# The first state of batches 1 to 7: its product with C moved from VectorE to ScalarE, behind the transposes, and the gate moved to step 1

## What is computed

```python
dA = jnp.exp(jnp.einsum('bti,is->btis', delta, A))
dBu = jnp.einsum('bti,bts->btis', delta * u, B_ssm)
def step(h, inp):
    dA_t, dBu_t, C_t = inp
    h = dA_t * h + dBu_t
    y_t = jnp.einsum('bis,bs->bi', h, C_t)
    return (h, y_t)
...
y = ys.transpose(1, 0, 2) + u * D_param
y = y * jax.nn.silu(z)
return y @ out_proj_w.T + residual
```

## Time and profile before

| what | us |
|---|---|
| median of 3 runs | 610.64 (609.68 to 610.68) |
| the profiled execution's own time | 611.13 |
| its span | 609.3 |
| DVE busy | 588.5 |
| PE busy | 542.0 |
| POOL busy | 494.1 |
| ACT busy | 455.0 |
| mean granted clock of PE | 0.969 of full speed |

### The profile page before, as it was taken

The page is one execution under the profiler, slowest core; times in us unless marked ns, Lnnn a source line. Parts: engine busy times, 40 slices in busy tenths (PEclk is TensorE's granted clock), DMA queues, the critical chain, the costliest instruction groups (busy, mean ns, idle before and its releaser), DMA issues.

```text
span 609.3 us, 11382 instructions
## 1 busy us (share of the span) xinstructions
PE 542.0 (89%) x3554; PEld 422.5 (69%) x3554; DVE 588.5 (97%) x852; ACT 455.0 (75%) x916; POOL 494.1 (81%) x389
## 2 busy tenths in 40 slices
PE   5999889898898998999989999899999797778887
PEld 2387766656787777877887777877777465657564
DVE  6999989999999999999999999999999998999997
ACT  1789697259857888579876698767985589969880
POOL 5693466569999799998999889998998967885784
PEclk9889798979999999999999999999999899988999
DMA  7430119725787887878868888688884455333364
GB/s 205 135 130 1 74 36 223 306 82 157 256 304 223 293 289 223 311 226 296 296 190 304 291 288 279 203 300 268 280 266 156 156 195 210 110 99 98 88 137 90
DMA packets 60893, 122.99 MB, mean 202 GB/s; under 512 B 8218, under 2 KB 41378, under 8 KB 53794
## 3 DMA queue, kind: packets, MB, share of 16 engines
q1 hardware_dynamic: 53826, 112.42, 54.7%
q0 software_dynamic: 6288, 9.52, 7.3%
q10 hardware_dynamic: 720, 0.33, 0.2%
HBM read 112.77 MB, written 9.47 MB: 201 GB/s over the span
## 4 chain that ended last, share of the span: by engine, by line
PE 50%; DVE 19%; ACT 16%; issue 13%; POOL 1%; DMA 1%; DVEq 0%; ACTq 0%; POOLq 0%
PE bank L1433 9%; PE bank L1584 8%; PE bank L1467 8%; DVE bank L1144 8%; PE bank L1598 6%; DVE h_sb L1161 6%; PE bank L1592 5%; ACT bank L515 3%; ACT dbu L531 3%; PE bank L1490 2%; ACT da L503 2%; PE bank L1482 2%; PE bank L1396 1%; PE bank L1565 1%; ACT L770 1%
## 5 line engine op out<-in xcount | busy, mean ns | idle before, releaser
L931 POOL TENSOR_TENSOR dbu<-du,xn_all 128x1024 f32<-128x1024 f32 x86 | 203.7, 2369 | 24.9 <-DVE bank L1144 21.5
L1144 DVE TENSOR_TENSOR_SCAN bank<-bank,dbu 128x512 f32<-128x512 f32 x170 | 207.4, 1222 | 0.8 <-ACT bank L515 0.2
L1161 DVE TENSOR_TENSOR h_sb<-bank,xh_all 128x512 f32<-128x512 f32 x240 | 159.6, 680 | 1.2
L515 ACT ACTIVATE bank<-delta,a_sb 128x512 f32<-128x512 f32 x170 | 116.7, 688 | 37.9 <-DVE h_sb L1161 37.2
L1433 PE MATMUL bank<-id_sb,h_sb 128*128 128x128 f32 x992 | 131.9, 277 | 10.9 <-DVE h_sb L1161 9.3
L1433 PEld LDWEIGHTS bank<-id_sb,h_sb 128*128 128x128 f32 x992 | 112.9, 143 | 21.6 <-DVE h_sb L1161 14.7
L1144 DVE TENSOR_TENSOR_SCAN bank<-da,bank 128x512 f32<-128x512 f32 x82 | 96.0, 1215 | 4.6 <-PE bank L1396 2.9
L1584 PEld LDWEIGHTS bank<-wd_sb,hid 117*128 117x128 f32 (+1 forms) x432 | 54.8, 191 | 49.2 <-DVE hid L1195 28.4
L1584 PE MATMUL bank<-wd_sb,hid 117*128 117x128 f32 (+1 forms) x432 | 64.1, 284 | 18.7 <-ACT xT L696 17.2
L915 POOL DMA_INDIRECT xs<-xn_rows,src x72 | 69.8, 970 | 12.5 <-issue 9.9
L531 ACT ACTIVATE dbu<-du_t,bc_sb 128x256 f32<-128x256 f32 x164 | 69.4, 496 | 6.3 <-PE bank L1396 3.4
(11 more groups left out here) (198 smaller groups left out, 893.8 us busy)
## 6 DMA issues: line engine op xcount, KB each, us to landing
xh_all<-b_rows SPq DMA_DIRECT2D x30, 1024.0 KB, 7.5
xn_all<-b_rows SPq DMA_DIRECT2D x25, 1024.0 KB
wgu_sb<-in_w_gu SPq DMA_DIRECT2D x72, 352.0 KB
wd_sb<-in_w_dn SPq DMA_DIRECT2D x72, 192.0 KB
y_slots<-ys SPq DMA_DIRECT2D x72, 64.0 KB
xn_rows<-xn_all SPq DMA_DIRECT2D x2, 1040.0 KB, 11.4
out<-x_sb SPq DMA_DIRECT2D x7, 256.0 KB, 7.0
x_sb<-in_x SPq DMA_DIRECT2D x2, 640.0 KB, 6.0
```

The costliest lines, as they stand in the source:

```text
L515: nc.scalar.activation(bank_of(b, m)[:, :], delta[b % 2][:, hf, :], ACT.Exp, scale=a_sb[:, hf, k:k + 1]).then_inc(s["da_rdy"], 1)
L931: nc.gpsimd.tensor_tensor(dbu[k % 2][:, :, :], du[b % 2][:, :, :], b_ring[c % 2][:, k % CH, :].unsqueeze(1).to_broadcast([P, NH, T]), ALU. ...
L1144: nc.vector.tensor_tensor_scan(at, da_of(n)[:, hf, :] if n in IN_SBUF else at, inp, 0.0, ALU.mult, ALU.add).then_inc(s["h_rdy"], 1)
L1161: nc.vector.tensor_tensor(h_sb[k % 2][:, hf, :], bank_of(b, 2 * k + hf)[:, :], row, ALU.mult).then_inc(s["p_rdy"], 1)
```

## The change

For step 0 of batches 1 to 7 (`BY_SCALAR`, n = 16b):

- The scan writes h_sb0 instead of its bank, and waits for that buffer at its start. The two products are not issued.
- PE turns the bare state into banks 2 and 3 with its first sums, and ACT multiplies the banks in place by C's column, four times 128x256 (`multiplied`), as the last work of its step 1. PE's sums of step 1 wait for that.
- The bank of such a step is free after its scan instead of after its product (`bank_read`).
- C's columns exist already for batches 6 and 7. For 1 to 5 PE turns them with four small transposes and ACT copies them (`own_columns`), in batch 0's step 7 and 8 for batch 1, and in front of one `slots_turn` of the batch before for the others.
- The gate stands in step 1, between its first scan with the expert product and its first product.
- On PE, the sums of steps 0 and 1 (issued in steps 1 and 2) stand behind gate and slots_turn in batches 1 to 5, and behind the next step's first dbu transposes in 6 and 7. In batch 6 the two halves of skip move from steps 1 and 2 to 2 and 3.

```diff
+        BY_SCALAR = [S * b for b in range(1, NB)]
+        def by_vector(m):
+            return m - sum(min(max(m - 2 * n, 0), 2) for n in BY_SCALAR)
+        def bank_read(eng, m):
+            if m > 0 and (m - 1) // 2 in BY_SCALAR:
+                wait(eng, "h_rdy", m)
+            else:
+                wait(eng, "p_rdy", by_vector(m))
...
-        SKIPPED = {6: (1, 2), 7: (2, 4)}
+        SKIPPED = {6: (2, 3), 7: (2, 4)}
+        COLUMN_TILE = {TILE[(b - 1) * S + (7 if b == 2 else 5)]: b for b in range(2, 6)}
...
-                wait(act, "p_rdy", freed(b, m))
+                bank_read(act, freed(b, m))
...
+                if g - 1 in BY_SCALAR:
+                    multiplied(g - 1)
...
+            def multiplied(n):
+                b, k = n // S, n % S
+                i0 = BY_SCALAR.index(n)
+                if 0 < b < 6:
+                    act.wait_ge(s["cc_rdy"], b)
+                for i in range(2):
+                    act.wait_ge(s["acc_mm"], 2 * n + i + 1)
+                    for t in (2 * i, 2 * i + 1):
+                        last = nc.scalar.activation(HT[i][:, t % 2, :], HT[i][:, t % 2, :], ACT.Copy,
+                                                    scale=bc_sb[b % 2][:, t, S + k:S + k + 1])
+                    last.then_inc(s["hc_rdy"], 1)
+            def own_columns(c):
+                act.wait_ge(s["cc_mm"], c)
+                at = XHB if c == 1 else XD
+                nc.scalar.activation(bc_sb[c % 2][:, :, S:S + 1], at[:, 2 * P:3 * P].rearrange("p (t c) -> p t c", t=TT)[:, :, S:S + 1],
+                                     ACT.Copy).then_inc(s["cc_rdy"], 1)
...
-                    wait(dve, "p_rdy", 2 * S * b + 1)
-                nc.vector.tensor_tensor_scan(at, da_of(n)[:, hf, :] if n in IN_SBUF else at, inp, 0.0,
+                    bank_read(dve, 2 * S * b + 1)
+                to = at
+                if n in BY_SCALAR:
+                    to = h_sb[k % 2][:, hf, :]
+                    wait(dve, "acc_mm", 2 * (n - 1))
+                nc.vector.tensor_tensor_scan(to, da_of(n)[:, hf, :] if n in IN_SBUF else at, inp, 0.0,
...
+                if b * S + k in BY_SCALAR:
+                    return
...
+                if k == 1:
+                    gate(b - 1)
                 product(b, k, 0)
...
-                if k == 0:
-                    gate(b - 1)
...
-                wait(pe, "p_rdy", 2 * (n + 1))
+                bank_read(pe, 2 * (n + 1))
...
+                    if n - 1 in BY_SCALAR:
+                        pe.wait_ge(s["hc_rdy"], 2 * BY_SCALAR.index(n - 1) + i + 1)
...
+                for t in range(TT):
+                    last = nc.tensor.transpose(at[:, 2 * P + t * 2 * S:2 * P + (t + 1) * 2 * S], bct_full[0:2 * S, t * P:(t + 1) * P],
+                                               id_sb[0:2 * S, 0:2 * S])
...
-                if k > 0:
+                if k > 2:
                     accumulate(g - 1)
                 if g + 1 in BY_PE:
                     dbu_turn(b, k + 1, (0,))
+                if k in (1, 2) and b > 5:
+                    accumulate(g - 1)
...
+                if k in (1, 2) and b < 6:
+                    accumulate(g - 1)
```

## The result

The changed kernel takes **617.52 us** (median of 5 runs, 615.92 to 619.37) beside 610.68 of the kernel before on the same chip (609.68 to 612.77): a ratio of **1.0107**, 95% interval 1.0083 to 1.0132. It is slower by 1%, where 610.3 us was forecast, with a range of 608.0 to 613.5. The profiled execution took 618.38 us, 616.6 of them span; before, the span was 609.3. The ratios of this document are those on record for kernels run side by side; they differ by up to 0.002 from the quotient of the two medians.

A forecast was written before the change was run, and what follows sets the result against it. VectorE, busy 97% of the span, was taken as the bound. Terms -1.25 - 2.1 + 0.5 + 2.5 = -0.35 us on the profiled 611.13 gave 610.3 us against the 610.64 median; range 608.0 to 613.5.

The forecast's parts named there:

- What goes: Fourteen products leave DVE, two in each of 7 batches: 1.55 us in batch 1, 1.18 in each other, 8.6 gross.
- the multiply's price: Four 128x256 multiplies per batch on ACT: 0.44 us alone, 0.36 in a row, 1.5 us per batch.
- Rival 3: Each multiply costs a full-width bank write, 0.6 us in a row, 2.4 per batch on ACT: 612.8 us; chance 0.10.
- Batch 1, -1.25 foreseen: Gross gain 1.55 us, less 0.3 for step 2's decay standing behind the multiplies on ACT; 1.25 left.
- first scan 121.24, gate 125.07: Batch 1's scan-to-gate time, 3.83 us against 2.25 to 2.28 for two scans back to back; gives batch 1's 1.55.
- Batches 2 to 5, -2.1 foreseen: Of 1.18 us per batch, waits for ACT's decays at steps 2, 5 and 10 leave 0.53, 2.1 for four.
- Batch 6, +0.5 foreseen: Late gate delays PE's queue; step 3's second scan gets its transposes at 495.1 instead of running at 494.67: 0.5 us lost.
- The wait of 1.2 for the decay: Batch 6, step 1: the scan waits 1.2 us at 483.4 for ACT's first decay, spending 0.68 of 1.18.
- rival 2: PE's clock falls in batch 6 after 1.5 us more waiting; 2.0 to 3.0 us added, 612.3 to 613.3; chance 0.18.
- Batch 7, +2.5 foreseen: Step 1's scan waits for ACT, and ACT's multiplies and scaled copies delay step 3's scans; 2.5 us lost, none regained.
- The wait of 2.4 for du's copies: Batch 7, second step: DVE arrives at 545.81 and waits 2.4 us while ACT empties bank 5 until 548.19.
- 0.4 for the half clock on the sums: Batch 7: PE at half clock in 552 to 554, as before the change, puts another 0.4 us on the sums.

The follow-up runs named there:

- e_sources: Changed kernel with VectorE's five small instructions on the sources in batch 1 moved behind step 1's gate; batch 1 took 71.10 us.
- e_nocol: Changed kernel without ScalarE's multiplies and without turning and copying C's column; batches 2, 3 and 4 took 72.49, 72.80 and 72.56 us, batch 7 67.11.
- e_thin: Changed kernel with six of eight matmuls left out of the sums of steps 0 to 2 in batches 2 to 5; batches 2 and 4 gave 0.64 us.
- e_last: The change in batches 6 and 7 alone, batches 0 to 5 as in the kernel before; 617.31 us, ratio 1.0120.

## Why the prediction was wrong

- **What goes, and the multiply's price: right.** 1.21 for the scan into SBUF, 226 products, multiplies of 438 ns and 1.51 in a row (0.44 and 1.5 foreseen); the moved gate waits nowhere in batches 2 to 5. Rival 3 is excluded.
- **Batch 1, -1.25 foreseen, -0.01 measured.** The step that failed is "first scan 121.24, gate 125.07": I costed scan, product and gate, and not the five instructions on the sources behind the gate. The change put them ahead of the gate and beside GpSimd's dbu, where one of them took 1.85 us more. And steps 10 and 14 take from batch 1 too (e_sources), where I let it go free after step 2.
- **Batches 2 to 5, -2.1 foreseen, +0.54 measured.** The places were right, steps 2, 5 and 10, and the sum of 0.65 was too small; it is 1.32 in batch 3. Step 5's first scan was to come 22.17 us after the batch's first (287.74 - 265.57) and came after 22.51 (287.57 - 265.06): 0.34 more, 0.30 of it C's column by e_nocol, put at zero because PE has 5 us of slack a batch. That slack is an average; in the 22 us to which the column was added PE has none. Step 5's second half was not costed, 0.28, though its decay stands in the same full row, and step 10 takes 0.35 to 0.46 for 0.3. Wrong too is the cause I gave for step 5, that ACT's row has no gap because of the multiplies: without them step 5 waits the same, and with them but with less work on PE (e_thin) it doesn't wait.
- **Batch 6, +0.5 foreseen, +2.43 measured.** The wait of 1.2 for the decay came (1.18). Where the half clock falls on y's turns, as before the change, the batch loses 0.8; the rest is rival 2, in its place (0.55 in 488 to 490) and with its signs, behind PE's pause of 3.25 us. That it struck in the profile is partly luck: e_sources, with the same code there, has 63.21. I gave the rival 0.18 and priced it for batch 6 alone. The page named with it, "TensorE: Matmul & The Clock Gate" of the Trainium skill, spoke against the change, and behind this pause the trace agrees with it.
- **Batch 7, +2.5 foreseen, +5.00 measured.** The wait of 2.4 for du's copies is 2.44. Counted from their batch's first scan, step 3's scans came 2.7 and 4.9 us late (561.19 - 545.86 against 556.18 - 543.56 for the first), where I had 1.0 and 2.1. I had 0.4 for the half clock on the sums, once. It struck the transposes and the sums twice, since each delay makes the pause ahead of the next stretch. And the step that let it cost so much is that ACT's multiplies wait for those sums ahead of the next scaled copies: without the multiplies the same half clock leaves the batch at 67.1 to 67.6.
- **The whole:** +8.0 us in the seven batches where -0.35 was foreseen; batch 0, whose end moves by more than that between executions, gave 0.66 back in this profile.
- **The rivals:** the range ended at 613.5 because rival 2 was worked out as one place. PE pauses some 3 us behind the changed order at three (3.25, 3.31 and 2.69).

## What to carry to other kernels

Ask of a freed microsecond which engine is next, at each step, from the row that engine runs without a pause, not from its share of busy time: here three rows on two engines took 1.2 us back, one after another. Look at every instruction that moves up because the one ahead of it went, and at what another engine does at the new time. Where a change makes TensorE pause, price the stretch behind the pause at half clock too, ask what waits for that stretch, and follow the delay round: if it makes the next pause, it is paid again. And before an edit is credited with a change of the clock, look whether the same code without the edit shows it in another execution.

## What the runs showed of the hardware

- A tensor_scalar of 72 columns took 2.05 us on DVE instead of 0.20 when GpSimd's tensor_tensor of 2.35 us had begun 0.34 us before it; a tensor_tensor of 72 columns beside the same instruction took 0.23.
- The same batch 6 was granted half clock in 482 to 486 in one execution (e_last) and in 488 to 492 in another (the changed kernel), with 1.6 us between them. The old batch 6 was granted half clock on y's turns in four of five executions and full speed in the fifth (1.68 to 1.97 and 1.09 us for the same eight transposes, behind the same pauses of 1.63 and 0.74 us).
- Half clock followed PE's pauses of 3.0 to 3.9 us at 550 to 556 in all eight executions without fill, and in none of the five in which fillers had cut that pause to 1.0 to 1.3 us.
- ScalarE writes a 128x256 product by a column back into the bank it reads in 438 ns, four in 1.51 us.
